# The last low weight part moved from GpSimd to VectorE, and the result copies moved ahead in the unit

## The chip, the cores and the metric

The kernel runs on one core of a Trainium2 chip. The metric is the device time of one execution in microseconds (us). The profile is that of one execution, in which the hardware recorded every instruction. Engines are named PE (TensorE), PEld (its weight loads), DVE (VectorE), ACT (ScalarE), POOL (GpSimd) and SP (the queue that issues transfers).

## The reference

The program is a graph attention layer over 625 nodes and 20000 edges, followed by a mixture of experts over the same 625 rows: each row goes to 2 of 8 experts (512 to 1024 to 512, gated by silu), and all rows through one shared expert. The change lies in the experts alone:

```python
def _L0_ffn_ref(x, gate_w, biases, w1, w3, w2, sw1, sw3, sw2):
    ...
    shared = jax.nn.silu(xt @ sw1) * (xt @ sw3) @ sw2
    scores = xt @ gate_w.T
    _, idx = jax.lax.top_k(scores + biases, K)
    topv, _ = jax.lax.top_k(scores, K)
    p = jax.nn.sigmoid(topv)
    p = p / jnp.sum(p, axis=-1, keepdims=True)
    h = jax.nn.silu(jnp.einsum('td,edh->eth', xt, w1)) * jnp.einsum('td,edh->eth', xt, w3)
    y = jnp.einsum('eth,ehd->etd', h, w2)
    onehot = jax.nn.one_hot(idx, E, dtype=xt.dtype)
    comb = jnp.einsum('tk,tke->te', p, onehot)
    out = jnp.einsum('te,etd->td', comb, y) + shared
    return out.reshape(Bb, Ss, D)
...
    x = x + _L0_ffn_ref(_layernorm(x, axis=-1)[None], L0_ffn_gate_w, L0_ffn_biases, L0_ffn_w1, L0_ffn_w3, L0_ffn_w2, L0_ffn_sw1, L0_ffn_sw3, L0_ffn_sw2)[0]
```

## The kernel before

Each matrix product is made from three products of rounded parts: a 32-bit operand is split into a high part (rounded to the fast matrix format, `fp32r`) and a low part (what the rounding left), and high x high, low x high and high x low are summed in PSUM. ScalarE makes a high part by copying, another engine the low part by subtracting the high part from the raw values.

`routed_units` computes the experts. Their rows stand in slots, at most `CAPS[r]` of them for the expert that comes in round r: 240, 224, 208, 192, 176, 160, 144 and 128, in blocks of 128 rows and the rest (one block in the last round). An expert is cut along its hidden size into `UNITS` = 4 units of `UW` = 256, so there are V = 32 units, v = 4r + u. A unit has three raw weight parts of 128 x 1024 values: two for the first products (w1, w3; numbers n = 0 and 1), one for the second product (w2, n = 2). After the 32 units one more set (v = V = 32) belongs to the rest of the shared expert.

The order on each engine is written out by hand, unit by unit, with semaphores between the engines:

- TensorE (L1831 to L1845): `up(v)` multiplies the rows with w1 and w3 for both halves m of the unit (L1784, L1786), then `down(v - 1)` adds the unit before to the expert's result with w2 (L1799), 12 products for two blocks of rows, 6 for one. In units with u = 2 `turn` (L1767) transposes the next expert's rows between the two. `down` of a unit with u = 0 opens a new result in PSUM, and so waits until the expert before has been copied out (L1796). Because `down(4r)` stands behind `up(4r + 1)`, that wait stands there too.
- ScalarE (L1739 to L1750): for the unit to come the high parts (L1699), for this one the sums moved out of PSUM (`low_part`, L1712), silu (`gate`, L1716) and the hidden values' high part (`high_hidden`, L1720, tile hidden_hi). In units with u = 2 also the next rows' high parts (L1704).
- VectorE (L1653 to L1668): `weights_lo` (L1601) makes the low parts of w1 and w3 of the next unit; `parts_summed` (L1614) adds PSUM to what ScalarE moved, `hidden` (L1618) multiplies the two gated factors, both in SBUF, `low_hidden` (L1622) makes the low part that `down` waits for. `rows_lo` (L1606) is the next rows' low part. `results` (L1629) copies the finished expert from PSUM, one copy for each block of rows.
- GpSimd (L1578 to L1582) makes the low part of w2. After the units it gathers each row's two results from memory by an indirect transfer (L1587).
- SP loads the next expert's unit u once the low parts of this expert's unit u have been made, since they free the raw buffer (L1560 to L1562):

```python
sp.wait_ge(w_lo_ready, 2 * (v + 1))
sp.wait_ge(w2_lo_ready, v + 1)
load_unit(sp, e, u, (w1, w3, w2), raw, raw_in)
```

Of the kernel before, what the change touches and what calls it, by code (L numbers as in the profile page):

```python
# [17 lines left out]
ALU = mybir.AluOpType  # L18
# [41 lines left out]
UNITS = HID // UW  # L60
# [1426 lines left out]
def routed_units(nc, block, sem, w1, w3, w2, sw1, sw3, sw2, rows_d, y_d, out, slots, xs, hT, rows_T, vs, gate_sb, most,  # L1487
# [10 lines left out]
    raw = routed_slots(slots)  # L1498
# [5 lines left out]
    V = EX * UNITS  # L1504
# [69 lines left out]
    @block.gpsimd  # L1574
    def _(pool):
        fullest = pool.value_load(most[0:1, 0:1], min_val=0, max_val=NP)
        with pool.If(fullest < CAP + 1):
            for v in range(V + 1):  # L1578
                u = v % UNITS
                pool.wait_ge(w_hi_ready, 3 * v + 3)  # L1580
                pool.tensor_tensor(w2s[u][1], raw_rest[2] if v == V else raw[u][2], w2s[u][0], ALU.subtract)\  # L1581
                    .then_inc(w2_lo_ready, 1)  # L1582
            for blk in range(CB):
                pool.wait_ge(y_out[blk], 16 * sum(len(slot_blocks(r)) > blk for r in range(EX)))
            for t in range(NT):
                for k in range(2):
                    pool.indirect_dma_start(  # L1587
                        out=got[k][:, t, :], out_offset=None, in_=y_d,
                        in_offset=bass.IndirectOffsetOnAxis(ap=slot_i[:, k, t:t + 1], axis=0))\
                        .then_inc(got_in[t], 16)  # L1590

    @block.vector
    def _(dve):
        fullest = dve.value_load(most[0:1, 0:1], min_val=0, max_val=NP)
        with dve.If(fullest < CAP + 1):
            def weights_lo(v, n):

                u = v % UNITS
                to = (w1s, w3s)[n][u % 2]
                dve.wait_ge(w_hi_ready, v * 3 + n + 1)  # L1600
                dve.tensor_tensor(to[1], raw_rest[n] if v == V else raw[u][n], to[0], ALU.subtract).then_inc(w_lo_ready, 1)  # L1601

            def rows_lo(r):
                dve.wait_ge(x_hi, r + 1)
                for blk, (s0, n) in enumerate(slot_blocks(r)):
                    last = dve.tensor_tensor(xT(r)[:, :, 1, s0:s0 + n], turned_bank(blk, n), xT(r)[:, :, 0, s0:s0 + n],  # L1606
                                             ALU.subtract)
                last.then_inc(x_lo, 1)

            def parts_summed(v, m):  # L1610

                cap = CAPS[v // UNITS]
                dve.wait_ge(a_low, v * UM + m + 1)
                dve.tensor_tensor(pair(v, m), pair(v, m), banks[:, 2 * m:2 * m + 2, 0:cap], ALU.add).then_inc(a_sum, 1)  # L1614
# [10 lines left out]
            def results(r):  # L1625
                for blk, (s0, n) in enumerate(slot_blocks(r)):
                    dve.wait_ge(y_ps, Y_DONE[r] + blk + 1)
                    wait_past(dve, y_out[blk], 16 * r)
                    dve.tensor_copy(y_st[blk][0:n, :], psum[4 + blk][0:n, :]).then_inc(y_sb, 1)  # L1629
# [21 lines left out]
                   .then_inc(rest_lo, 1)  # L1651

            rows_lo(0)  # L1653
            for n in range(2):
                weights_lo(0, n)
            for v in range(V):
                r, u = v // UNITS, v % UNITS
                weights_lo(v + 1, 0)
                parts_summed(v, 0)
                weights_lo(v + 1, 1)  # L1660
                hidden(v, 0)
                if u == 1 and r:
                    results(r - 1)
                parts_summed(v, 1)
                if u == 2 and r + 1 < EX:
                    rows_lo(r + 1)
                hidden(v, 1)
                low_hidden(v)  # L1668
            rest_hidden(0, 0)
# [10 lines left out]
            for t in range(NT):  # L1680
                n = P if t < NT - 1 else LAST
# [527 lines left out]
```

## Time and profile before

| | us |
|---|---|
| median of 3 runs (lowest, highest) | 856.68 (854.65, 857.11) |
| the profiled execution | 855.59 |
| its span in the trace | 854.0 |
| TensorE busy | 767.4 (90%) |
| VectorE busy | 554.9 (65%) |
| ScalarE busy | 460.8 (54%) |
| GpSimd busy | 301.0 (35%) |

The span is the trace from first to last instruction; the profiled execution's own time is 1.6 us longer, and the median of the runs 1.1 us longer than that. The units of the experts lie between 549 and 825 us of the span. Busy shares are means over the whole program, whose stages have different limits; a stage is read from its own stretches and waits.

### The profile page before, as it was taken

To read this page: it belongs to the slowest core of one execution; us is meant where nothing else is said; L and a number is where in the kernel's file an instruction comes from. 1 tells how busy PE (TensorE), PEld (TensorE's weight loads), DVE (VectorE), ACT (ScalarE), POOL (GpSimd) and SP (SyncE) were. 2 spreads that over 40 slices of the span, in tenths; PEclk is the share of its full clock that TensorE was granted. 3 is DMA by queue.
4 is the path that set the end of the run, shared out by engine and by line. 5 is a ranking of instruction groups with operands and counts; after the bars stand their busy time and mean duration, and the time that the engine had idled before them with its cause. 6 is when DMAs were issued, how large, how long until landed. Compare 5 with 4: busy or idle time off the path is not lost. (4 is left out here: it accounts for less than half of the span.)

```text
span 854.0 us, 13328 instructions
## 1 busy us (share of the span) xinstructions
PE 767.4 (90%) x4993; PEld 640.5 (75%) x4993; DVE 554.9 (65%) x904; ACT 460.8 (54%) x748; POOL 301.0 (35%) x189
## 2 busy tenths in 40 slices
PE   3997799999999978899996999799889899898894
PEld 2664588787878753899995999688788787786784
DVE  6628997979797926454226444478686786777755
ACT  4244596868686825633334332356565665566530
POOL 8240686868686820000000004033222222232333
PEclk9999799999999989899998699999999999999998
DMA  9320830000000006000004208756565766556015
GB/s 260 119 41 9 298 67 2 1 2 2 1 2 2 1 9 251 1 1 1 2 0 152 71 1 297 249 175 224 174 237 193 231 207 210 194 196 218 34 37 162
DMA packets 66460, 92.46 MB, mean 108 GB/s; under 512 B 6723, under 2 KB 44197, under 8 KB 65877
## 3 DMA queue, kind: packets, MB, share of 16 engines
q1 hardware_dynamic: 64149, 85.77, 30.9%
q0 software_dynamic: 2240, 5.76, 2.2%
q8 instruction: 43, 0.70, 0.3%
q14 instruction: 28, 0.23, 0.1%
HBM read 80.69 MB, written 10.82 MB: 107 GB/s over the span
## 5 line engine op out<-in xcount | busy, mean ns | idle before, releaser
L1581 POOL TENSOR_TENSOR w_lo<-weights_far,w_hi 128x1024 fp32r<-128x1024 f32 x32 | 77.0, 2406 | 210.9 <-ACT w_hi L1699 210.9
L660 POOL TENSOR_TENSOR bias_exp_hi<-edge_exp_hi,mask 128x640 fp32r<-128x640 f32 x40 | 98.0, 2451 | 71.3 <-PE ps L806 32.3
L1784 PE MATMUL ps<-xT,w_hi 128*128 128x480 f32 (+7 forms) x512 | 112.1, 342 | 3.6 <-DVE w_lo L1601 3.6
L1784 PEld LDWEIGHTS ps<-xT,w_hi 128*128 128x128 f32 x512 | 84.6, 194 | 9.9 <-issue 4.1
L1786 PEld LDWEIGHTS ps<-xT,w_lo 128*128 128x128 f32 x512 | 74.7, 192 | 1.7
L1786 PE MATMUL ps<-xT,w_lo 128*128 128x240 f32 (+7 forms) x512 | 75.4, 270 | 0.0
L806 PE MATMUL ps<-onehot,bias_exp_hi 128*128 128x314 f32 x400 | 69.5, 320 | 5.4 <-POOL bias_exp_hi L660 5.0
L1799 PE MATMUL ps<-w_hi,hidden_hi 128*128 128x512 f32 (+7 forms) x120 | 52.1, 434 | 23.0 <-DVE weights_near L1629 21.0
L1618 DVE TENSOR_TENSOR hT<-hT 128x240 f32<-128x240 f32 (+7 forms) x64 | 63.2, 988 | 11.3 <-ACT hT L1716 11.3
L1699 ACT ACTIVATE w_hi<-weights_far 128x1024 fp32r<-128x1024 f32 x64 | 67.1, 1050 | 0.0
L806 PE MATMUL ps<-onehot,bias_exp_lo 128*128 128x314 f32 x400 | 65.7, 311 | 0.0
L806 PEld LDWEIGHTS ps<-onehot,bias_exp_hi 128*128 128x128 f32 x400 | 59.4, 193 | 6.5 <-POOL bias_exp_hi L660 5.2
L660 POOL TENSOR_TENSOR bias_exp_lo<-edge_exp_lo,mask 128x640 fp32r<-128x640 f32 x40 | 61.8, 1544 | 0.0
L806 PEld LDWEIGHTS ps<-onehot,bias_exp_lo 128*128 128x128 f32 x400 | 60.6, 192 | 0.7 <-issue 0.7
L675 DVE TENSOR_SCALAR onehot<-iota_n,records 128x628 fp32r<-128x628 f32 x84 | 60.7, 730 | 0.0
L680 DVE TENSOR_TENSOR onehot<-iota_n,records 128x1256 fp32r<-128x1256 f32 x38 | 56.8, 1495 | 4.7 <-PE ps L806 1.9
L964 DVE TENSOR_TENSOR ff_hidden_lo<-ff_hidden,ff_hidden_hi 128x640 fp32r<-128x640 f32 x16 | 13.2, 825 | 69.1 <-ACT ff_hidden_hi L1016 69.1
L1601 DVE TENSOR_TENSOR w_lo<-weights_near,w_hi 128x1024 fp32r<-128x1024 f32 x34 | 43.4, 1277 | 12.8 <-ACT w_hi L1699 12.8
L816 PE MATMUL ps<-queries,keys 128*32 128x314 f32 x640 | 50.6, 433 | 0.4 <-ACT exponents L758 0.4
L1013 ACT ACTIVATE ff_hidden<-ps,vs 128x320 f32<-128x320 f32 x32 | 16.9, 528 | 61.5 <-PE ps L1065 61.5
L1799 PE MATMUL ps<-w_lo,hidden_hi 128*128 128x512 f32 (+7 forms) x120 | 49.9, 416 | 0.0
L1799 PE MATMUL ps<-w_hi,hidden_lo 128*128 128x512 f32 (+7 forms) x120 | 49.8, 415 | 0.0
(272 smaller groups left out, 1678.8 us busy)
## 6 DMA issues: line engine op xcount, KB each, us to landing
weights_far<-in_L_ffn_w SPq DMA_DIRECT2D x64, 512.0 KB, 5.5
weights_near<-in_L_ffn_w SPq DMA_DIRECT2D x32, 512.0 KB, 3.6
weights_near<-in_L_gnn_W SPq DMA_DIRECT2D x1, 4096.0 KB, 14.5
weights_near<-in_L_gnn_Wqkv SPq DMA_DIRECT2D x3, 1024.0 KB, 8.2
weights_ff<-in_L_gnn_W SPq DMA_DIRECT2D x1, 3072.0 KB, 13.9
weights_lo_shared<-in_L_ffn_sw SPq DMA_DIRECT2D x6, 512.0 KB, 7.7
weights_near<-in_L_ffn_sw SPq DMA_DIRECT2D x6, 512.0 KB, 6.7
slot_rows<-zeros SPq DMA_DIRECT2D x1, 2944.0 KB, 26.1
```

Source lines behind the costliest of these rows:

```text
L660: pool.tensor_tensor(to.rearrange("p t (h d) -> p t h d", h=H), e[:, b, :, :].unsqueeze(3).broadcast_to([P, CT, H, BN]), m.unsqueeze(2).br ...
L675: dve.tensor_scalar(onehot[b % 2][:, t, :], iota_n[:, 0:SRC], rec[:, b, t, 0:1], None, ALU.is_equal).then_inc(oh_ready, 1)
L680: dve.tensor_tensor(onehot[b % 2][:, 0:2, :], iota_n[:, 0:SRC].unsqueeze(1).broadcast_to([P, 2, SRC]), rec[:, b, 0:2, 0:1].broadcast_to([P ...
L806: last = pe.matmul(psum[2 * k + a][:, 0:SH], r[:, t, :], onehot[k][:, t, a * SH:(a + 1) * SH], start=t == 0 and part == 0, stop=t == CT - ...
L816: last = pe.matmul(psum[4 + a][c * 2 * BN:(c + 1) * 2 * BN, 0:SH], KB[:, c, b, :], qT[:, c, a * SH:(a + 1) * SH], start=True, stop=True)
L1581: pool.tensor_tensor(w2s[u][1], raw_rest[2] if v == V else raw[u][2], w2s[u][0], ALU.subtract)\
L1601: dve.tensor_tensor(to[1], raw_rest[n] if v == V else raw[u][n], to[0], ALU.subtract).then_inc(w_lo_ready, 1)
L1618: dve.tensor_tensor(unit_hidden(h32_all, v)[:, m, :], pair(v, m)[:, 0, :], pair(v, m)[:, 1, :], ALU.mult) .then_inc(h_made, 1)
L1699: act.activation(to[0], raw_rest[n] if v == V else raw[u][n], ACT.Copy).then_inc(w_hi_ready, 1)
L1784: pe.matmul(both(bank, cap), w[u % 2][0][:, c, cut], xT(r)[:, c, :, :], start=c == 0, stop=False)
L1786: last = pe.matmul(bank[:, 0:cap], w[u % 2][1][:, c, cut], xT(r)[:, c, 0, :], start=False, stop=c == DC - 1)
L1799: last = pe.matmul(psum[4 + blk][0:rows, :], unit_hidden(hid_all[hp], v)[:, m, s0:s0 + rows], w2s[u][wp][:, m, :], start=u == 0 and m == 0 ...
```

## The change

GpSimd's loop over the units goes. `weights_lo` now also makes the low part of w2 (n = 2), in each unit behind the second addition (and the next rows' low part) and ahead of the second product, and counts it on the semaphore `w2_lo_ready` as GpSimd did. The copies of `results(r - 1)`, in units with u = 1, move from behind the first product to ahead of the first addition.

```diff
--- before.py
+++ after.py
@@ -1575,11 +1575,6 @@
     def _(pool):
         fullest = pool.value_load(most[0:1, 0:1], min_val=0, max_val=NP)
         with pool.If(fullest < CAP + 1):
-            for v in range(V + 1):
-                u = v % UNITS
-                pool.wait_ge(w_hi_ready, 3 * v + 3)
-                pool.tensor_tensor(w2s[u][1], raw_rest[2] if v == V else raw[u][2], w2s[u][0], ALU.subtract)\
-                    .then_inc(w2_lo_ready, 1)
             for blk in range(CB):
                 pool.wait_ge(y_out[blk], 16 * sum(len(slot_blocks(r)) > blk for r in range(EX)))
             for t in range(NT):
@@ -1596,9 +1591,10 @@
             def weights_lo(v, n):
 
                 u = v % UNITS
-                to = (w1s, w3s)[n][u % 2]
+                to = ((w1s, w3s)[n][u % 2] if n < 2 else w2s[u])
                 dve.wait_ge(w_hi_ready, v * 3 + n + 1)
-                dve.tensor_tensor(to[1], raw_rest[n] if v == V else raw[u][n], to[0], ALU.subtract).then_inc(w_lo_ready, 1)
+                dve.tensor_tensor(to[1], raw_rest[n] if v == V else raw[u][n], to[0], ALU.subtract)\
+                   .then_inc(w_lo_ready if n < 2 else w2_lo_ready, 1)
 
             def rows_lo(r):
                 dve.wait_ge(x_hi, r + 1)
@@ -1651,19 +1647,20 @@
                    .then_inc(rest_lo, 1)
 
             rows_lo(0)
-            for n in range(2):
+            for n in range(3):
                 weights_lo(0, n)
             for v in range(V):
                 r, u = v // UNITS, v % UNITS
                 weights_lo(v + 1, 0)
+                if u == 1 and r:
+                    results(r - 1)
                 parts_summed(v, 0)
                 weights_lo(v + 1, 1)
                 hidden(v, 0)
-                if u == 1 and r:
-                    results(r - 1)
                 parts_summed(v, 1)
                 if u == 2 and r + 1 < EX:
                     rows_lo(r + 1)
+                weights_lo(v + 1, 2)
                 hidden(v, 1)
                 low_hidden(v)
             rest_hidden(0, 0)
```

VectorE, unit 4r + 1 of round 1 (u = 1; the copies are of expert 0), before. L1601 is `weights_lo`, L1614 the addition, L1618 the product, L1622 the low hidden part, L1629 the copies:

```order
L1601 TENSOR_TENSOR w_lo<-weights_near,w_hi 128x1024
L1614 TENSOR_TENSOR hT<-hT,ps 128x448
L1601 TENSOR_TENSOR w_lo<-weights_far,w_hi 128x1024
L1618 TENSOR_TENSOR hT<-hT 128x224
L1629 COPY weights_near<-ps 128x512
L1629 COPY weights_near<-ps 112x512
L1614 TENSOR_TENSOR hT<-hT,ps 128x448
L1618 TENSOR_TENSOR hT<-hT 128x224
L1622 TENSOR_TENSOR hidden_lo<-hT,hidden_hi 128x448
```

and now, where these are L1596, L1610, L1614, L1618 and L1625:

```order
L1596 TENSOR_TENSOR w_lo<-weights_near,w_hi 128x1024
L1625 COPY weights_near<-ps 128x512
L1625 COPY weights_near<-ps 112x512
L1610 TENSOR_TENSOR hT<-hT,ps 128x448
L1596 TENSOR_TENSOR w_lo<-weights_far,w_hi 128x1024
L1614 TENSOR_TENSOR hT<-hT 128x224
L1610 TENSOR_TENSOR hT<-hT,ps 128x448
L1596 TENSOR_TENSOR w_lo<-weights_far,w_hi 128x1024
L1614 TENSOR_TENSOR hT<-hT 128x224
L1618 TENSOR_TENSOR hidden_lo<-hT,hidden_hi 128x448
```

The copies stand three rows earlier, behind the first subtraction, and a third subtraction stands ahead of the second product.

VectorE, unit 4r + 2 of round 1 (u = 2), where the next rows' low parts (L1606, now L1602) stand, before:

```order
L1601 TENSOR_TENSOR w_lo<-weights_near,w_hi 128x1024
L1614 TENSOR_TENSOR hT<-hT,ps 128x448
L1601 TENSOR_TENSOR w_lo<-weights_far,w_hi 128x1024
L1618 TENSOR_TENSOR hT<-hT 128x224
L1614 TENSOR_TENSOR hT<-hT,ps 128x448
L1606 TENSOR_TENSOR xT<-ps,xT 128x4x128
L1606 TENSOR_TENSOR xT<-ps,xT 128x4x80
L1618 TENSOR_TENSOR hT<-hT 128x224
L1622 TENSOR_TENSOR hidden_lo<-hT,hidden_hi 128x448
L1601 TENSOR_TENSOR w_lo<-weights_near,w_hi 128x1024
```

and now:

```order
L1596 TENSOR_TENSOR w_lo<-weights_near,w_hi 128x1024
L1610 TENSOR_TENSOR hT<-hT,ps 128x448
L1596 TENSOR_TENSOR w_lo<-weights_far,w_hi 128x1024
L1614 TENSOR_TENSOR hT<-hT 128x224
L1610 TENSOR_TENSOR hT<-hT,ps 128x448
L1602 TENSOR_TENSOR xT<-ps,xT 128x4x128
L1602 TENSOR_TENSOR xT<-ps,xT 128x4x80
L1596 TENSOR_TENSOR w_lo<-weights_far,w_hi 128x1024
L1614 TENSOR_TENSOR hT<-hT 128x224
L1618 TENSOR_TENSOR hidden_lo<-hT,hidden_hi 128x448
L1596 TENSOR_TENSOR w_lo<-weights_near,w_hi 128x1024
```

The third subtraction follows the next rows' low parts.

GpSimd, from the stage's branch to the first gather, before:

```order
L1577 COMPARE_AND_BRANCH
L1581 TENSOR_TENSOR w_lo<-weights_far,w_hi 128x1024 x32
L1581 TENSOR_TENSOR w_lo<-weights_near,w_hi 128x1024
L1587 DMA weights_far<-slot_results,gate 128x512
```

and now:

```order
L1577 COMPARE_AND_BRANCH
L1582 DMA weights_far<-slot_results,gate 128x512
```

The subtractions, 33 in two rows, are gone; the gathers follow at once, behind the wait for the stored results.

## Rows read from the trace of the kernel before

**Rows 1.** Stretches: start:end, length; busy PE, PEld, DVE, ACT, POOL; clock; DMA share; GB/s.

```profile
520.00:560.00 40.00, 34.52 (x184) 30.95 (x182) 18.50 (x30) 11.29 (x18) 8.87 (x7) 0.91 0.82 284
650.00:700.00 50.00, 47.36 (x286) 41.86 (x285) 38.75 (x49) 30.03 (x50) 14.96 (x7) 1.00 0.65 209
```

**Rows 2.** Waits, 553 to 826 us: who waited, total us, times, longest us.

```profile
ACT hidden_hi L1720 <- DVE hT L1618: 60.5, 32, 2.5
...
PE ps L1799 <- DVE weights_near L1629: 21.0, 7, 3.6
```

**Rows 3.** TensorE in time order: start, duration us; in brackets idle before, releaser.

```profile
587.17 0.98 PE L1784 MATMUL ps<-xT,w_hi 128*128 128x448 f32 x4
...
592.23 0.40 PE L1799 MATMUL ps<-w_hi,hidden_hi 128*128 128x512 f32 x1
...
595.02 0.97 PE L1784 MATMUL ps<-xT,w_hi 128*128 128x448 f32 x4
...
599.63 0.60 PE L1786 MATMUL ps<-xT,w_lo 128*128 128x224 f32 x4
603.65 0.76 PE L1799 MATMUL ps<-w_hi,hidden_hi 128*128 128x512 f32 x1 [3.42 <-DVE weights_near L1629]
...
608.04 0.97 PE L1784 MATMUL ps<-xT,w_hi 128*128 128x448 f32 x4
```

**Rows 4.** The chain that ended last: start us, us, what.

```profile
639.33 3.02 PE ps L1799 x12
...
706.06 4.54 PE ps L1799 x12
...
804.79 2.74 PE ps L1799 x6
```

**Rows 5.** All engines in time order, one unit of round 1.

```profile
590.25 0.61 ACT L1720 ACTIVATE hidden_hi<-hT 128x480 fp32r<-128x480 f32 x1 [2.17 <-DVE hT L1618]
...
591.84 1.23 DVE L1601 TENSOR_TENSOR w_lo<-weights_near,w_hi 128x1024 fp32r<-128x1024 f32 x1 [0.29 <-ACT w_hi L1699]
...
592.98 0.61 DVE L1614 TENSOR_TENSOR hT<-hT,ps 128x448 f32<-128x448 f32 x1
...
593.51 1.22 DVE L1601 TENSOR_TENSOR w_lo<-weights_far,w_hi 128x1024 fp32r<-128x1024 f32 x1
...
594.64 0.38 DVE L1618 TENSOR_TENSOR hT<-hT 128x224 f32<-128x224 f32 x1
...
594.95 0.61 DVE L1614 TENSOR_TENSOR hT<-hT,ps 128x448 f32<-128x448 f32 x1
...
595.47 2.40 POOL L1581 TENSOR_TENSOR w_lo<-weights_far,w_hi 128x1024 fp32r<-128x1024 f32 x1 [5.53 <-ACT w_hi L1699]
...
596.02 2.10 DVE L1618 TENSOR_TENSOR hT<-hT 128x224 f32<-128x224 f32 x1 [0.46 <-ACT hT L1716]
...
598.15 0.58 ACT L1720 ACTIVATE hidden_hi<-hT 128x448 fp32r<-128x448 f32 x1 [2.16 <-DVE hT L1618]
```

**Rows 6.** Line L1618, whole span: duration ns min/median/max.

```profile
L1618 DVE TENSOR_TENSOR hT<-hT x64: 280/401/2428, 561.5 to 820.6; 128x240 f32<-128x240 f32 x8, 128x224 f32<-128x224 f32 x8, 128x208 f32<-128x208 f32 x8, 128x192 f32<-128x192 f32 x8
```

**Rows 7.** Time order at the last expert: TensorE, then ScalarE and VectorE.

```profile
784.28 0.70 PE L1784 MATMUL ps<-xT,w_hi 128*128 128x288 f32 x4
...
790.93 0.63 PE L1784 MATMUL ps<-xT,w_hi 128*128 128x256 f32 x4
...
794.56 0.45 PE L1799 MATMUL ps<-w_hi,hidden_hi 128*128 128x512 f32 x1
...
823.73 0.50 PE L1799 MATMUL ps<-w_hi,hidden_hi 128*128 128x512 f32 x1 [1.64 <-DVE hidden_lo L1622]
...
792.57 0.44 ACT L1720 ACTIVATE hidden_hi<-hT 128x288 fp32r<-128x288 f32 x1 [2.20 <-DVE hT L1618]
...
796.81 0.41 DVE L1614 TENSOR_TENSOR hT<-hT,ps 128x256 f32<-128x256 f32 x1
...
799.76 0.42 ACT L1720 ACTIVATE hidden_hi<-hT 128x256 fp32r<-128x256 f32 x1 [2.19 <-DVE hT L1618]
```

## The prediction

> **What bounds the kernel now.** I read first the busy time by stage, then the waits of the expert stage, then the instructions in order of time around one long wait and inside one unit. In 650 to 700 us TensorE is busy 47.4 of 50 us at a granted clock of 1.00, VectorE 38.8, and the transfers take 0.65 of the DMA engines [rows 1]: TensorE paces the units, but VectorE is near. The waits [rows 2] show where they meet: TensorE stood 21.0 us in 7 waits for the copies of L1629, and ScalarE 60.5 us in 32 waits for the products of L1618.
>
> The long wait, at the second unit of expert round 1 [rows 3]: a unit costs TensorE 5.06 us for the first two weights (587.17 to 592.23) and 2.79 for the third (592.23 to 595.02), 7.85 together. After its next first part (the last group starts at 599.63) it stands 3.42 us for the copy, and then takes 4.39 us (603.65 to 608.04) for twelve products that took 2.79 before. The first of them lasted 0.76 us where its counterpart took 0.40, which is the 1.2 GHz level against 2.4. So this place costs 3.4 and 1.6 us. In the chain [rows 4] the twelve products after a wait cost 4.54 in one round and 3.02 in another: the waits of 2.3 and 2.6 us (two of the seven) leave the clock up, the other five don't. In the last round there are six products, 2.74 us, where 1.4 would do. In all: 21.0 us of waits and 5 x 1.6 = 8.0 us of slow clock.
>
> Why the copy is late [rows 5]: this is a unit of VectorE. Unit 4's first part ended on TensorE at 592.23, yet VectorE adds its second half at 594.95, over 2 us late. It is late because the loop between ScalarE and VectorE takes 7.90 us (590.25 to 598.15), longer than TensorE's 7.85. What fills it is the second product of L1618: 2.10 us, when the first took 0.38. GpSimd's subtraction starts at 595.47 and ends at 597.87; the product ends 0.25 us behind it. Over the whole stage L1618 takes 401 ns in the median and 2428 at most [rows 6]. The additions of L1614, which read PSUM, are not drawn out.
>
> **The change, part by part.** (a) GpSimd's 33 subtractions of 2.40 us go. Nothing waited for them but the queue of loads and, in the tail, nothing: there GpSimd waits for the stored results. Their gain is what they take off VectorE: the product falls from 2.10 to 0.38, 1.7 us in each unit.
>
> (b) VectorE gets 33 subtractions of the same shape and operands as its own at 593.51, 1.22 us each, starting 1.13 to 1.14 before the next instruction. The new loop is read off the same unit [rows 5], from hidden_hi's start at T = 590.25: the second addition stands at T+4.70; the new subtraction can follow at T+5.24 (its high part is there, since GpSimd starts at 595.47, T+5.22); the product at T+6.37, done at T+6.75; hidden_hi at T+6.8. So **6.8 us in place of 7.90** (1.7 less, 1.1 more, and 0.5 less since the subtraction fills the idle 0.46 us before the product), against TensorE's 7.85: VectorE is ahead by 1 us a unit. For the last expert [rows 7]: T = 792.57, second addition T+4.24, subtraction T+4.57, product T+5.71 with 0.28 us (the shortest of L1618 [rows 6]), hidden_hi at T+6.0, where it was 7.19. TensorE needs 3.63 (790.93 to 794.56) and 1.4, so 5.0: **in the last round VectorE is the bound**. In round 6 TensorE takes 6.65 (784.28 to 790.93), VectorE 6.1, plus 1.2 once for the copies and about 1.5 once for the next expert's rows, whose high and low parts now stand one after the other ahead of the third subtraction: 4 x 6.1 + 2.7 = 27.1 against TensorE's 4 x 6.65 + 0.5 for turning rows = 27.1. The two are even there; earlier TensorE's units are longer. I take a lag of 0.35 us into the last round, with 0 and 1.5 as its ends.
>
> The trace shows that each drawn-out product ends just behind GpSimd's instruction, not what would happen without one. The Trainium skill (SBUF — State Buffer, "Who interferes with whom") states that a VectorE instruction with two SBUF inputs contends with a GpSimd one that reads SBUF, and that the loser is blocked for the whole instruction. By it the product falls back to 0.38 us as I take it; without it 2.10 us would stay, the second rival's case.
>
> (c) The copies move ahead of the first addition. They would now wait there for the down products of the expert before, and everything of VectorE's unit is queued behind them. Let U be the end of the first part of unit 4r. Those down products end at U+2.8. VectorE reaches the copy after: addition by U+1.2, third subtraction U+1.5 to U+2.75, product to U+3.0, hidden_hi, the next high part, the first subtraction; in round 1 that gives the copy at U+5.8 to U+6.5, in the last round U+5.5 to U+6.2. So it doesn't wait itself. TensorE wants it at U+7.85 in round 1 and at U+6.5 in the last: no wait, with a margin that shrinks from 1.3 us to about nothing. The 1.2 us that the copies take delay the additions behind them, which TensorE wants only a unit later.
>
> (d) The loads wait for the third low part too; it is now there at about 596.7 where it was 597.87, so they go out no later. A shorter round asks more of them: 6.3 MB of weights in 27 us is 233 GB/s, where 209 are moved now and 284 were at the stage's start [rows 1]; and a unit's load is issued some three units ahead. I cost it at nothing; were that cover gone, TensorE would wait for the difference, 6.3 MB at 209 GB/s being 30 us a round. (e) The extra subtraction before unit 0 lies in VectorE's idle time while TensorE does its first unit: nothing.
>
> **The sum.** Up to the last round TensorE no longer waits: six waits, 21.0 - 3.6 = 17.4 us, and four of the five slow stretches, 6.4: **23.8 us**. In the last round, from U = 794.56 to the last down products at 823.73 it takes 29.2 us now [rows 7]. After: hidden_hi of unit 28 at U+2.9+0.35, then 7.2 (with copies), 6.0, 6.0, and 0.9 to the low part that TensorE waits for: 23.4. **5.8 us**. Together 29.6. The tail behind that point (store, gathers, output) moves as it is. The profiled execution took 855.6 us, so 826.0; the median of the runs is 1.1 us above it: **827.1 us**.
> Ends: were TensorE never waiting in the last round, its own work is 2.8 + 3 x 3.63 + 3 x 1.4 + 3.5 (two groups of the shared part) = 21.4 us, gaining 7.8 in place of 5.8: 825. With a lag of 1.5 us and a half-microsecond wait per round, 831.
>
> **The rivals.** *VectorE is the bound all along.* The Trainium skill (Perfetto Trace Analysis, "Optimizing Scalar/DVE Operations") advises to take work off VectorE when it is saturated, even to GpSimd, which speaks against this move. In rows: VectorE has 38.8 of 50 us busy now, GpSimd 15.0 [rows 1]. For it: the two are even in round 6, and the wait for the next rows' high parts now holds up a subtraction. Against: 2.2 us of blocking and idling go for 1.1 of work. Were each VectorE unit 0.4 us longer than I read it, the loop would pass TensorE's time from round 3 on: 5 rounds x 4 x 0.4 = 8 us given back, 835. A wait of about 1 us left at each of the seven places, with the clock kept, gives 7 back: 834.
> *Slower: the long product is not GpSimd's doing.* Then 2.10 us stay and 1.14 come on top: 9.04 us a unit in round 1 and 8.33 in the last, always above TensorE's 7.85. Round 1 would take 4 x 9.04 + 1.2 = 37.4 us where it takes 35.7 from copy to copy (603.65 to 639.33 [rows 3, 4]), and rounds 4 to 6, at 8.6 us a unit, 35.6 each where they take 32.9 (706.06 to 804.79, by three [rows 4]). With 1.7 to 2.7 us more a round, 2.4 x 8 = 19 us: 876. It decides once the product keeps more than some 1.5 us, for then the loop is above TensorE's time again. Against it: each long product ends a quarter of a microsecond behind GpSimd, the first product of the same unit, with GpSimd idle, never is long.
> *The clock stays down.* If TensorE's slow stretches had another cause than the waits, 8 us don't come back: 835. Against: each starts at or just behind a wait, and the two shortest waits have none.
> *The copy waits itself* and stalls VectorE: only if VectorE ran ahead of TensorE by 2.7 us, which its place behind the product of unit 4r excludes.
>
> **How the numbers follow.** Forecast (825 to 831) 0.65, VectorE as bound 0.22, clock 0.05, better than 825 0.03, no gain because the two cancel 0.02, slower 0.03. The range reaches from 823.5 (the best case, less the scatter of a run) to 836 (both partial cases). 0.3%, some 2.6 us, is about what a measurement of this kernel can tell from no change: faster by more 0.95, within 0.02, slower by more 0.03.
>
> **What would show it.** In the changed profile: the product line without any instance over 0.5 us; three subtractions of 1.2 us per unit on VectorE; no wait of TensorE for the copies, or under 0.5 us; granted clock near 1.00 from 560 us to the end of round 6; hidden_hi to hidden_hi 6.0 us in the last round, TensorE waiting there for low parts. Wrong: products of 2 us, waits for the copy over 1 us, TensorE waiting for third low parts or loads in the early rounds.

## The result and the profile after

| | before | changed |
|---|---|---|
| median (lowest, highest), us | 856.89 (854.65, 857.95) | 827.31 (827.11, 828.45) |
| ratio, 95% interval | | 0.9661 (0.9640, 0.9682) |
| the profiled execution, us | 855.59 | 827.11 |
| its span | 854.0 | 825.4 |
| busy: TensorE, VectorE, GpSimd | 767.4, 554.9, 301.0 | 763.2, 546.9, 221.3 |

The changed kernel is 29.6 us faster; 827.1 was forecast. Lines 1577 and later have moved up: `weights_lo` is now L1596, `rows_lo` L1602, the addition L1610, the product L1614, the low hidden part L1618, the copies L1625; on ScalarE hidden_hi is L1717, on TensorE the second products are L1796.

Two stretches of the changed kernel, to be held against [rows 1] (busy PE, PEld, DVE, ACT, POOL; clock; DMA share; GB/s):

```profile
650.00:700.00 50.00, 50.00 (x308) 44.26 (x307) 40.71 (x60) 33.70 (x56) 0.00 (x0) 1.00 0.70 230
700.00:750.00 50.00, 50.00 (x326) 42.86 (x325) 40.40 (x63) 34.31 (x60) 0.00 (x0) 1.00 0.73 242
```

TensorE is busy all of the 50 us, in each of them, at a granted clock of 1.00. VectorE has 40.7 of 50 us, 2 more than before, though it has one more instruction of 1.22 us in a unit. The transfers run at 230 and 242 GB/s: the faster rounds asked for it, and no wait of TensorE in them is for a load.

The waits of the same stage, to be held against [rows 2]:

```profile
ACT hidden_hi L1717 <- DVE hT L1614: 44.6, 32, 2.7
...
PE ps L1796 <- DVE hidden_lo L1618: 0.5, 1, 0.5
...
PE ps L1796 <- DVE weights_near L1625: 0.2, 1, 0.2
```

Of TensorE's 21.0 us for the copies 0.2 are left, of its 1.6 for the last low hidden part 0.5. The product of VectorE over the whole span (ns, min/median/max), against [rows 6]:

```profile
L1614 DVE TENSOR_TENSOR hT<-hT x64: 273/342/404, 563.3 to 792.9; 128x240 f32<-128x240 f32 x8, 128x224 f32<-128x224 f32 x8, 128x208 f32<-128x208 f32 x8, 128x192 f32<-128x192 f32 x8
```

None of the 64 is drawn out: 404 ns at most, where it was 2428. In the kernel before, 31 of the 32 second products of a unit end 0.15 to 0.27 us behind GpSimd's subtraction; the other one starts after it and takes 0.40 us. They are not all as long as the one in [rows 5]: in the units with copies it takes about 0.9 us, in those with the next rows 0.4 to 1.3, in the others 2.1 to 2.4. One with copies, of the kernel before:

```profile
605.08 0.87 DVE L1618 TENSOR_TENSOR hT<-hT 128x224 f32<-128x224 f32 x1 [0.46 <-ACT hT L1716]
```

There GpSimd had begun at 603.34 and was nearly through.

Inside one unit, all engines in order of time, from one hidden_hi to the next, the counterpart of [rows 5]:

```profile
589.53 0.61 ACT L1717 ACTIVATE hidden_hi<-hT 128x480 fp32r<-128x480 f32 x1 [1.05 <-DVE hT L1614]
...
591.12 1.23 DVE L1596 TENSOR_TENSOR w_lo<-weights_near,w_hi 128x1024 fp32r<-128x1024 f32 x1 [0.29 <-ACT w_hi L1696]
...
592.26 0.61 DVE L1610 TENSOR_TENSOR hT<-hT,ps 128x448 f32<-128x448 f32 x1
...
592.79 1.22 DVE L1596 TENSOR_TENSOR w_lo<-weights_far,w_hi 128x1024 fp32r<-128x1024 f32 x1
...
593.93 0.39 DVE L1614 TENSOR_TENSOR hT<-hT 128x224 f32<-128x224 f32 x1
...
594.24 0.61 DVE L1610 TENSOR_TENSOR hT<-hT,ps 128x448 f32<-128x448 f32 x1
...
594.78 1.23 DVE L1596 TENSOR_TENSOR w_lo<-weights_far,w_hi 128x1024 fp32r<-128x1024 f32 x1
...
595.92 0.39 DVE L1614 TENSOR_TENSOR hT<-hT 128x224 f32<-128x224 f32 x1
...
596.34 0.58 ACT L1717 ACTIVATE hidden_hi<-hT 128x448 fp32r<-128x448 f32 x1 [1.07 <-DVE hT L1614]
```

From 589.53 to 596.34 is 6.81 us; it was 7.90. The third subtraction (594.78) stands in the place where GpSimd's began, VectorE goes through without a gap, and the product at 595.92 takes 0.39 us.

The last expert, against [rows 7]:

```profile
774.04 0.42 ACT L1717 ACTIVATE hidden_hi<-hT 128x256 fp32r<-128x256 f32 x1 [1.05 <-DVE hT L1614]
...
777.41 0.47 PE L1796 MATMUL ps<-w_hi,hidden_hi 128*128 128x512 f32 x1 [0.18 <-DVE weights_near L1625]
...
781.24 0.42 ACT L1717 ACTIVATE hidden_hi<-hT 128x256 fp32r<-128x256 f32 x1 [1.05 <-DVE hT L1614]
...
787.25 0.42 ACT L1717 ACTIVATE hidden_hi<-hT 128x256 fp32r<-128x256 f32 x1 [1.04 <-DVE hT L1614]
...
793.27 0.42 ACT L1717 ACTIVATE hidden_hi<-hT 128x256 fp32r<-128x256 f32 x1 [1.05 <-DVE hT L1614]
...
794.20 0.50 PE L1796 MATMUL ps<-w_hi,hidden_hi 128*128 128x512 f32 x1 [0.49 <-DVE hidden_lo L1618]
```

ScalarE's hidden_hi comes after 7.20 us in the unit with the copies, then after 6.01 and 6.02: here VectorE sets the pace. TensorE stands 0.18 us for the copy and 0.49 for the last low part. That is not all: its weight loads also wait, for an addition and for a low weight part, and hold up the products behind them:

```profile
784.25 0.53 PEld L1781 LDWEIGHTS ps<-xT,w_hi 128*128 128x128 f32 x4 [0.58 <-DVE hT L1610]
...
789.93 0.59 PEld L1811 LDWEIGHTS ps<-sh_rows_hi,w_hi 128*128 128x128 f32 x4 [0.52 <-DVE w_lo L1596]
```

Where the time came from can be read off TensorE's own marks in the two traces. From its first product of the stage (553.57 before, 555.35 now) to the last down products (823.73, 794.20) it takes 270.2 us before and 238.9 now: 31.3 less. The parts, by the end of each round's third unit: 0.9 before the first copy, then 5.2, 2.5, 2.8, 4.5, 4.8 and 5.0 for the six waits up to the last round, 5.6 in it. In these two executions the stage began 1.8 us later and the tail took 0.9 us more; so the spans differ by 28.6. Other executions below enter the stage at 552.3 to 556.9 us with the same program ahead of it, and their tails take 30.7 to 32.4 us (30.3 before, 31.2 here): both look like scatter.

The part that repeats lies between TensorE's first second products (567.37 before, 568.34 now) and its last: 256.4 us before, 225.86 now, and 225.87 and 225.88 in two other traces with the same work on TensorE and VectorE (`after_again` and `pool_write` below). That is 30.5 us less. The other 0.8 us stand ahead of it. There 0.39 are a wait for a low hidden part, and the other 0.4 lie mostly in when the clock rose in the first unit, which is scatter too: this stretch takes 12.99 us here and 12.39 in another execution of the same kernel.

### The profile page after: what moved, and what is told of

Read it like the earlier page. It is cut to its first block and busy times, and to the rows that moved or that the text cites. A ratio compares the mean times of both kernels' runs of the same rounds, so it can differ in the third digit from the quotient of the medians.

```text
span 825.4 us, 13328 instructions
## 1 busy us (share of the span) xinstructions
PE 763.2 (92%) x4993; PEld 638.0 (77%) x4993; DVE 546.9 (66%) x937; ACT 461.9 (56%) x748; POOL 221.3 (27%) x156
## 5 line engine op out<-in xcount | busy, mean ns | idle before, releaser
L1596 DVE TENSOR_TENSOR w_lo<-weights_far,w_hi 128x1024 fp32r<-128x1024 f32 x64 | 78.0, 1219 | 3.1 <-ACT w_hi L1696 2.7
L1582 POOL DMA_INDIRECT weights_far<-slot_results,gate x5 | 5.1, 1017 | 271.4 <-DMA slot_results<-weights_near 270.2
L1596 DVE TENSOR_TENSOR w_lo<-weights_near,w_hi 128x1024 fp32r<-128x1024 f32 x35 | 42.9, 1225 | 12.5 <-ACT w_hi L1696 12.5
L1796 PE MATMUL ps<-w_hi,hidden_hi 128*128 128x512 f32 (+7 forms) x120 | 48.8, 407 | 0.7 <-DVE hidden_lo L1618 0.5
L1796 PE MATMUL ps<-w_hi,hidden_lo 128*128 128x512 f32 (+7 forms) x120 | 47.2, 393 | 0.0
L1796 PE MATMUL ps<-w_lo,hidden_hi 128*128 128x512 f32 (+7 forms) x120 | 47.1, 392 | 0.0
```

The costliest lines, as they stand in the source:

```text
L1796: last = pe.matmul(psum[4 + blk][0:rows, :], unit_hidden(hid_all[hp], v)[:, m, s0:s0 + rows], w2s[u][wp][:, m, :], start=u == 0 and m == 0 ...
```

## The experiments

Each is an edit of the changed kernel unless it says otherwise. The times are medians, the ratios are to the kernel before on the same chip, run in turn with them, with their 95% intervals. Short names used below: w2_only (the third subtraction alone), copy_only (the place of the copies alone), copy_mid, no_third, pool_read, pool_write, dve_extra (one more instruction), old_memset (the kernel before without GpSimd's reading), after_again (the changed kernel once more).

### The third subtraction alone

```diff
                 weights_lo(v + 1, 0)
-                if u == 1 and r:
-                    results(r - 1)
                 parts_summed(v, 0)
                 weights_lo(v + 1, 1)
                 hidden(v, 0)
+                if u == 1 and r:
+                    results(r - 1)
                 parts_summed(v, 1)
```

> Only the third subtraction moves to VectorE; the copies stay behind the first product. Theory (the loop of ScalarE and VectorE is shortened from 7.9 to 6.8 us, and lags TensorE no more): TensorE still waits for the copies, which now come only by their place too late: in each of seven rounds 1.3 to 1.8 us in place of 2.3 to 3.6, short enough that the clock stays up. 21 us faster than before, 836. No product of VectorE over 0.5 us. Rival (the place of the copies is the whole gain): waits of 2 us or more, slow clock behind them, under 10 us gained, 847 or more.

Measured: 837.0 us, 0.9765 (0.9731 to 0.9800), 21.3 us under the 858.3 of the kernel before. TensorE's wait for the copies, the first of seven and the last (start, duration; in brackets the idle time before):

```profile
599.79 0.47 PE L1796 MATMUL ps<-w_hi,hidden_hi 128*128 128x512 f32 x1 [1.31 <-DVE weights_near L1625]
...
786.66 0.62 PE L1796 MATMUL ps<-w_hi,hidden_hi 128*128 128x512 f32 x1 [1.74 <-DVE weights_near L1625]
```

They run 1.31, 1.37, 1.44, 1.53, 1.61, 1.69, 1.74, 10.7 us in all, and behind the first six all twelve products take 0.39 to 0.47 us: the clock stays up. Behind the last it is down (0.62 and 0.63 us), which was not expected. So the copies in their old place are late by that place alone. Ahead of the first wait:

```profile
595.98 0.55 ACT L1709 ACTIVATE hT<-ps 128x448 f32<-128x448 f32 x1 [0.68 <-PE ps L1783]
...
598.95 1.28 DVE L1625 COPY weights_near<-ps 128x512 f32<-128x512 f32 x2
```

ScalarE waits for the first half of the unit's first products on TensorE, and starts at 595.98. Behind it stand an addition, a subtraction and a product, so the copies begin 3.0 us later. TensorE needs only 2.5 us for the second half and then wants the copy (598.48). In smaller experts its half gets shorter faster than that chain does, and the wait grows. The rest of the old waits was VectorE's lag.

### The place of the copies alone

```diff
-            for n in range(3):
+            for n in range(2):
                 weights_lo(0, n)
...
                     rows_lo(r + 1)
-                weights_lo(v + 1, 2)
                 hidden(v, 1)
```
with GpSimd's loop as it was before.

> Only the copies move; GpSimd keeps the third subtraction. Theory: the loop stays at 7.9 to 7.2 us, so VectorE lags TensorE more the smaller the expert; the wait for the copies falls to 0.8 to 1.3 us in rounds 1 to 3, grows back to 2.5 to 3 in rounds 5 and 6, and in the last round TensorE also waits for low parts. About 11 us gained, 846. Rival (the place of the copies is the whole gain): 828 to 832, no wait over 1 us.

Measured: 845.4 us, 0.9855 (0.9824 to 0.9885), 12.9 us under 858.3. The product on VectorE, and TensorE's shortest and longest wait for the copies:

```profile
L1619 DVE TENSOR_TENSOR hT<-hT x64: 271/401/2406, 563.3 to 809.6; 128x240 f32<-128x240 f32 x8, 128x224 f32<-128x224 f32 x8, 128x208 f32<-128x208 f32 x8, 128x192 f32<-128x192 f32 x8
```

```profile
635.91 0.47 PE L1800 MATMUL ps<-w_hi,hidden_hi 128*128 128x512 f32 x1 [0.84 <-DVE weights_near L1630]
...
792.49 0.76 PE L1800 MATMUL ps<-w_hi,hidden_hi 128*128 128x512 f32 x1 [2.89 <-DVE weights_near L1630]
```

The products are drawn out as before. The waits are 1.47, 0.84, 1.03, 1.50, 1.97, 1.54 and 2.89 us, and in the last round TensorE also stands for low parts. The early rounds gain, and the lag comes back as the experts get smaller, as expected; but round 1 waits more (1.47 us, 1.3 at most expected) and rounds 5 and 6 less (1.97 and 1.54, where 2.5 to 3 were expected). The two parts alone give 21.3 and 12.9 us; together 29.6 were measured. They share some of it, as one would expect where one removes the lag and the other gives it more room.

### The copies two instructions later

```diff
                 weights_lo(v + 1, 0)
-                if u == 1 and r:
-                    results(r - 1)
                 parts_summed(v, 0)
                 weights_lo(v + 1, 1)
+                if u == 1 and r:
+                    results(r - 1)
                 hidden(v, 0)
```

> The changed kernel with the copies two instructions later (behind the second subtraction, ahead of the first product). Theory (the copy has a margin of 1.3 us in round 1 that shrinks to nothing in the last): 1.8 us later brings waits of about 0.5 us in round 1 up to 1.8 in the last, 7 us slower than the changed kernel, 834 to 835. Rival (any place before the old one is early enough, the lag was the cause): 827 to 829.

Measured: 833.6 us, 0.9731 (0.9700 to 0.9761). TensorE's first and last of the seven waits:

```profile
599.46 0.47 PE L1796 MATMUL ps<-w_hi,hidden_hi 128*128 128x512 f32 x1 [1.00 <-DVE weights_near L1625]
...
784.82 0.47 PE L1796 MATMUL ps<-w_hi,hidden_hi 128*128 128x512 f32 x1 [1.53 <-DVE weights_near L1625]
```

8.9 us in seven waits. The size is as expected, its spread is not: the first wait is 1.00 us, not 0.5. In this place too the copies stand behind an addition that needs the first half of the same unit on TensorE. They start at 598.63, only 0.3 us earlier than with the old place (598.95), which is what the product took that they passed. The margin is lost by this dependence, not only by the 1.8 us of work in between.

### No third low part

```diff
-            for n in range(3):
+            for n in range(2):
                 weights_lo(0, n)
...
-                weights_lo(v + 1, 2)
+                if v + 1 == V:
+                    weights_lo(v + 1, 2)
```
TensorE and the queue of loads then wait for `w_hi_ready` in place of `w2_lo_ready`.

> The changed kernel without the low part of the third weight in the 32 units: nobody makes it, and TensorE multiplies by the high part in its place (the output lacks that part). Theory (TensorE bounds rounds 0 to 6, VectorE the last): VectorE has 1.1 us less per unit, which is worth nothing but in the last round, 1.5 to 2.5 us: 825. Rival (VectorE is the bound in more of the rounds): each round gains, 8 us or more, 819 or less.

Measured: 825.5 us, 0.9632 (0.9604 to 0.9660). The waits of the expert stage in it, and TensorE's first product of the stage and its last down products:

```profile
ACT hidden_hi L1718 <- DVE hT L1614: 20.0, 32, 1.5
...
PE ps L1782 <- DVE w_lo L1596: 3.6, 1, 3.6
```

```profile
554.61 1.94 PE L1782 MATMUL ps<-xT,w_hi 128*128 128x480 f32 x4 [3.60 <-DVE w_lo L1596]
...
791.44 0.63 PE L1797 MATMUL ps<-w_hi,hidden_hi 128*128 128x512 f32 x2
```

In this stage TensorE waits for nothing but its first weights, so this is what it takes when TensorE alone sets it: 236.8 us (554.61 to 791.44), where the changed kernel's profiled execution has 238.9. From the first second products on it is 223.86 against 225.86, and all of the 2.0 us lie in the last round. The medians differ by 1.8 us, and their intervals overlap. 32 subtractions of 1.22 us, 39 us of VectorE's work, cost some 2 us of the kernel's time. A bound by VectorE in more of the rounds would have shown as 8 us or more.

### What drew the product out

GpSimd has nothing to do in the changed kernel's units. Two kernels give it something again, on a table (iota_n) that is dead by then, at the moment at which it used to subtract. In the first it reads and writes SBUF:

```diff
+            for v in range(V + 1):
+                pool.wait_ge(w_hi_ready, 3 * v + 3)
+                for k in range(2):
+                    wait_past(pool, extra, 2 * v + k)
+                    pool.tensor_tensor(iota_n[:, 0:512], iota_n[:, 0:512], iota_n[:, 0:512], ALU.subtract).then_inc(extra, 1)
             for blk in range(CB):
```

> The changed kernel, but GpSimd has two subtractions of 512 values again at the moment of its old one, on a table that nobody needs any more: nothing waits for it but the gathers at the end. Theory (a GpSimd instruction that reads SBUF holds off VectorE's with two SBUF inputs, and is not itself waited for by anyone): VectorE's third subtraction or the product behind it ends only after GpSimd's, the loop grows by up to 2.4 us to about 9 us and VectorE becomes the bound everywhere: far slower than before, 865 to 890, the lower end if the two engines alternate. Rival (the long product had its cause in the order, or in the data that both read): 827 to 829.

Measured, in one run: 844.3 us, beside 857.2 of the kernel before. The same unit of round 1 on GpSimd and on VectorE, and the product over the whole span:

```profile
596.07 3.27 POOL L1583 TENSOR_TENSOR iota_n<-iota_n 128x512 f32<-128x512 f32 x2 [4.36 <-ACT w_hi L1702]
```

```profile
596.07 1.22 DVE L1602 TENSOR_TENSOR w_lo<-weights_far,w_hi 128x1024 fp32r<-128x1024 f32 x1
...
597.20 1.23 DVE L1620 TENSOR_TENSOR hT<-hT 128x224 f32<-128x224 f32 x1
```

```profile
L1620 DVE TENSOR_TENSOR hT<-hT x64: 272/386/1247, 562.1 to 808.6; 128x240 f32<-128x240 f32 x8, 128x224 f32<-128x224 f32 x8, 128x208 f32<-128x208 f32 x8, 128x192 f32<-128x192 f32 x8
```

Slower than the changed kernel by 17 us, with work that nobody waits for. So the order and the data of the old subtraction were not the cause. But I had its size wrong, 865 to 890: I took it that GpSimd would go first. Both start at 596.07 and VectorE's subtraction keeps its 1.22 us; the product, which starts when that subtraction is done, takes 1.23 in place of 0.39. GpSimd's pair takes 3.27 us, and only 2.16 in a unit in which VectorE works with inputs from PSUM meanwhile:

```profile
579.03 2.16 POOL L1583 TENSOR_TENSOR iota_n<-iota_n 128x512 f32<-128x512 f32 x2 [4.44 <-ACT w_hi L1702]
```

The loop, from hidden_hi at 590.84 to the next at 598.46, takes 7.62 us in place of 6.81: it grows by 0.8 and not by 2.4. The records fit engines that take turns: whoever begins first goes through, and the other waits for its end, inside the time that the profile shows as busy.

In the second GpSimd only writes, four times, for about the same time:

```diff
...
+                for k in range(4):
+                    wait_past(pool, extra, 4 * v + k)
+                    pool.memset(iota_n[:, 0:512], 0.0).then_inc(extra, 1)
```

```profile
591.75 2.29 POOL L1583 MEMSET iota_n<- 128x512 f32 x4 [4.58 <-ACT w_hi L1702]
```

```profile
591.72 1.23 DVE L1602 TENSOR_TENSOR w_lo<-weights_far,w_hi 128x1024 fp32r<-128x1024 f32 x1
592.86 0.39 DVE L1620 TENSOR_TENSOR hT<-hT 128x224 f32<-128x224 f32 x1
```

```profile
L1620 DVE TENSOR_TENSOR hT<-hT x64: 272/342/404, 560.2 to 789.9; 128x240 f32<-128x240 f32 x8, 128x224 f32<-128x224 f32 x8, 128x208 f32<-128x208 f32 x8, 128x192 f32<-128x192 f32 x8
```

VectorE's subtraction and product run inside GpSimd's 2.29 us of writing and keep their 1.23 and 0.39 us. The Trainium skill (SBUF — State Buffer, "Who interferes with whom") says just this: a VectorE instruction with two SBUF inputs contends with a GpSimd one that reads SBUF, not with one that only writes it. Both halves of the rule are borne out here, 1247 against 404 ns at most.

### One more instruction on VectorE

```diff
                 parts_summed(v, 1)
+                wait_past(dve, extra, v)
+                dve.tensor_tensor(iota_n[:, 0:512], iota_n[:, 0:512], iota_n[:, 0:512], ALU.subtract).then_inc(extra, 1)
```

> The changed kernel with one more VectorE instruction per unit, a subtraction of 512 values on a table that nobody needs (0.69 us), behind the second addition. Theory (VectorE is ahead of TensorE by 1 us a unit in round 1, even with it in round 6, behind in round 7): nothing lost before round 1, copy waits that grow from 0.5 to 2 us, about 10 us slower than the changed kernel, 837. Rival (TensorE is the bound with room everywhere): 827 to 830. Rival (VectorE is the bound everywhere): 32 x 0.6 = 19 us, 846.

Measured: 836.7 us, 0.9755 (0.9733 to 0.9778). TensorE's shortest wait for the copies (round 2) and its longest (the last):

```profile
633.82 0.47 PE L1799 MATMUL ps<-w_hi,hidden_hi 128*128 128x512 f32 x1 [0.40 <-DVE weights_near L1626]
...
785.39 0.77 PE L1799 MATMUL ps<-w_hi,hidden_hi 128*128 128x512 f32 x1 [2.07 <-DVE weights_near L1626]
```

The waits are 0.80, 0.40, 0.47, 0.81, 1.12, 1.51 and 2.07 us: from round 2 on they grow as the experts shrink, and none of the seven rounds is free of one. The time is as expected: 0.7 us more a unit costs 9.4 us, and not 32 x 0.6. The room is smaller than the 1 us that was read off one unit, since that unit has neither copies nor next rows. An estimate by rounds, from hidden_hi to hidden_hi: round 1 takes 32.3 us here; less four times 0.58 (what the extra instruction adds to a loop, 7.39 in place of 6.81) this is 30.0, where TensorE's round takes 31.9 in the changed kernel. In round 6 it is 26.6 against 26.8. So VectorE has some 0.5 us a unit in round 1, and next to nothing in round 6.

### The kernel before without GpSimd's reading

An edit of the kernel before: GpSimd fills the low part with zeros where it subtracted. Nothing moves to VectorE, and the copies stay in the old place.

```diff
-                pool.tensor_tensor(w2s[u][1], raw_rest[2] if v == V else raw[u][2], w2s[u][0], ALU.subtract)\
-                    .then_inc(w2_lo_ready, 1)
+                if v == V:
+                    pool.tensor_tensor(w2s[u][1], raw_rest[2], w2s[u][0], ALU.subtract).then_inc(w2_lo_ready, 1)
+                else:
+                    for k in range(2):
+                        last = pool.memset(w2s[u][1][:, k, :].bitcast(F32), 0.0)
+                    last.then_inc(w2_lo_ready, 1)
```

> The kernel before, in its order, except that GpSimd fills the third low part of the 32 units with zeros (two memsets of 512 values) where it subtracted: the output lacks that part, nothing is added to VectorE, and GpSimd no longer reads SBUF. Theory (what drew out the second product was GpSimd's reading, and the copies wait by their place alone once VectorE keeps up): products under 0.5 us, the seven waits at 1.3 to 1.8 us as in w2_only, 21 us faster than the kernel before, so moving the subtraction onto VectorE costs nothing until the last round. Rival (much of w2_only's gain came from the new order on VectorE): waits of 2 us or more, under 12 us gained.

Measured: 837.7 us, 0.9776 (0.9750 to 0.9803), 19.9 us under 857.6. The product over the span, TensorE's first wait for the copies, and the one place where GpSimd still subtracts:

```profile
L1622 DVE TENSOR_TENSOR hT<-hT x64: 283/348/2140, 560.4 to 800.4; 128x240 f32<-128x240 f32 x8, 128x224 f32<-128x224 f32 x8, 128x208 f32<-128x208 f32 x8, 128x192 f32<-128x192 f32 x8
```

```profile
599.75 0.47 PE L1803 MATMUL ps<-w_hi,hidden_hi 128*128 128x512 f32 x1 [1.31 <-DVE weights_near L1633]
...
799.99 2.39 POOL L1582 TENSOR_TENSOR w_lo<-weights_near,w_hi 128x1024 fp32r<-128x1024 f32 x1 [4.21 <-ACT w_hi L1703]
...
800.38 2.14 DVE L1622 TENSOR_TENSOR hT<-hT 128x128 f32<-128x128 f32 x1 [0.38 <-ACT hT L1720]
```

The median product is back at 348 ns, and the wait is 1.31 us, the same as with the third subtraction on VectorE; the other six agree with that run to 0.01 us. The one long product left (800.38, 2.14 us) stands beside the one subtraction left to GpSimd. So the 20 us of the first half of the change are the end of the blocking; that VectorE does the work itself costs nothing that can be measured beside it.

### Earlier still

The copies ahead of the first subtraction; and, in a second kernel, also the third subtraction ahead of the next rows' low parts:

```diff
+                if u == 1 and r:
+                    results(r - 1)
                 weights_lo(v + 1, 0)
-                if u == 1 and r:
-                    results(r - 1)
...
+                weights_lo(v + 1, 2)
                 if u == 2 and r + 1 < EX:
                     rows_lo(r + 1)
-                weights_lo(v + 1, 2)
```

> The changed kernel itself, as the measure for the two beside it on the same chip: 826 to 828.5, ratio to the kernel before 0.965 to 0.967.

> The changed kernel with the copies one instruction earlier still, ahead of the first subtraction. Theory (VectorE idles there some 0.3 to 0.5 us until ScalarE has written the high part, while the expert's result has long been there; rounds 0 to 6 are TensorE's anyway): only the last round gains, the copy wait of 0.2 us, the low parts' 0.6 and part of the later units, about 1 us: 826. Rival (the copy would now wait for the down products and hold everything up): slower, 830 or more. Rival (nothing left to gain, within what the measurement can tell): the same within 0.1%.

> As copy_first, and the third subtraction ahead of the next rows' low parts in the third unit, so that VectorE doesn't wait for ScalarE with work at hand. Theory: that wait lies in rounds that TensorE bounds, so no gain over copy_first: 826. Rival (VectorE enters the last round late because of it): 1 to 2 us faster than copy_first, 824 to 825.

Measured side by side: the changed kernel 827.4 us, 0.9612 (0.9593 to 0.9631); copies first 826.8, 0.9601 (0.9575 to 0.9627); with the subtraction ahead too 826.4, 0.9601 (0.9583 to 0.9619). The intervals overlap, so the gain of up to 1 us is not shown by the times. TensorE's first product of the stage and its last down products, of the changed kernel and of copies first:

```profile
555.98 1.54 PE L1781 MATMUL ps<-xT,w_hi 128*128 128x480 f32 x3 [3.60 <-DVE w_lo L1596]
...
794.24 0.50 PE L1796 MATMUL ps<-w_hi,hidden_hi 128*128 128x512 f32 x1 [0.48 <-DVE hidden_lo L1618]
```

```profile
556.91 1.54 PE L1781 MATMUL ps<-xT,w_hi 128*128 128x480 f32 x3 [3.60 <-DVE w_lo L1596]
...
794.21 0.50 PE L1796 MATMUL ps<-w_hi,hidden_hi 128*128 128x512 f32 x1 [0.49 <-DVE hidden_lo L1618]
```

The stage takes 238.3 us and 237.3, and the copy wait of 0.18 us is gone. From the first second products on it is 225.87 and 224.93, and three traces of the unchanged order agree there to 0.02 us: so the 1 us expected is in the traces, while the scatter ahead of the stage and in the tail hides it in the times. The swap gains next to nothing more (224.86; the stage 237.2). The ratio of the changed kernel is lower beside these two than at first (0.9612 against 0.9661) because the kernel before, run in turn with them, took 860.8 us; its own time is the same to 0.1 us. That ratio was expected at 0.965 to 0.967.

## Why the prediction was right

- **What bounds the kernel.** TensorE, held up in seven places: shown by the stage's 100% busy slices after, and by the kernel without a third low part, where it is held nowhere behind its first weights and gains only some 2 us more.
- **(a) the product falls from 2.10 to 0.38 us.** 0.39 measured in the same unit, 0.40 at most in any. This step rested on the Trainium skill's rule and on where the products end; the pair of kernels with GpSimd reading and writing, and the old order without its reading, now show it. But "1.7 us in each unit" was too much: it holds where neither copies nor next rows stand in the unit, and over the 32 units the old trace has 41 us of it, 1.3 a unit. The sum did not use this term; it went by TensorE's waits.
- **(b) the loop of 6.8 us, 6.0 in the last round.** 6.81, 6.01 and 6.02. Adding up the starts of one unit of the old trace was exact to 0.02 us, since the same instructions stand in the same order up to the new one. The 1 us a unit that it leaves VectorE is that of a unit without copies and next rows; the forecast counted both for round 6 alone (27.1 us on either engine, measured some 26.6 and 26.8).
- **(c) the copy's place.** The forecast margin of 1.3 us falling to nothing: no wait in rounds 1 to 6, 0.18 us in the last. With U as in the forecast, the copy starts at U+6.00 in round 1 (599.05) and at U+5.96 in the last (776.58), inside both ranges. It gave the mechanism only in part. What makes the old place late even without lag is that it stands behind an addition and a product that depend on the first half of the same unit on TensorE; the middle place has the same flaw and costs 6.3 us.
- **(d) the loads** cost nothing: 233 GB/s were reckoned, 230 and 242 moved in the two stretches, 255 from 700 to 725 us.
- **The sum.** Up to the last round 23.8 us forecast, 25.7 measured; in it 5.8 and 5.6. The 1.9 us more are two things left out: 0.9 us in round 0, where TensorE also waited 0.39 us for a low hidden part and its clock rose later, and 0.1 to 0.2 us at each wait besides its idle time. The two executions differ by 31.3 us in the stage and by 28.6 in the span; the medians differ by 29.6. For the profiled execution the forecast was 826.0 and 827.11 came, 1.1 us off; and the median lies 0.2 us above it, not 1.1. That the forecast meets the median to 0.2 us is luck: the terms left out, the scatter outside the stage and the step from profile to median cancel. The kernel before scatters more than the changed one, 854.7 to 861.7 us over all its executions, and the longer ones mostly have the lower mean granted clock (855.4 at 0.958, 858.3 at 0.953, 861.7 at 0.950). Whether more of its seven waits lose the clock there is not shown, since only one of its executions has a trace.
- **The rivals.** VectorE as the bound all along: only in the last round, and the extra instruction shows how near the others are: some 0.5 us a unit in round 1, next to nothing in round 6. The slower case, the long product not being GpSimd's: refuted; no run shows its price of 876 us. The clock staying down: it is 1.00 from 600 to 790 us now, and every slow stretch of the second products is gone with its wait.

## What to carry to other kernels

A vector instruction whose duration has two modes may be waiting inside its busy time; look which engine's instruction ends just before it does, and compare one that reads PSUM. Work moved from GpSimd onto a VectorE that looks 78% busy can be free, when part of that busy time is blocking by the very instruction that moves, and when the loop behind it has room against the engine that bounds. A copy that frees a buffer for the bounding engine came in time here only ahead of the instructions that depend on that engine's current unit. Both things are read off one unit written out in order of time; how much room is left has to be added up over a whole round.

## What the runs showed that I had not expected

Both engines pay for contention, in turns: in a unit without copies and next rows two short GpSimd instructions cost VectorE 0.85 us and themselves 1.1 (3.27 in place of 2.16, by GpSimd's own spans), where the one of 2.4 us, which began first, cost VectorE 1.7.

How long TensorE waited does not alone say what the clock does behind the wait. Of the waits for the copies, those of 1.74 us in w2_only and old_memset were followed by products of 0.62 and 0.63 us, the 1.2 GHz level, and so were those of 1.97 (copy_only), 2.07 (dve_extra), 2.21 and 2.24 us (pool_read); one of 1.94 in pool_read left them at 0.39, and in the kernel before 2.29 and 2.64 us did. None up to 1.69 us lowered the clock in these runs, every one from 2.79 us on did, at once or a few products later. The forecast took it that the two shortest of the old waits keep the clock, which was right for those seven and would not have been for others.
